# Final layer norm of a mixture-of-experts kernel: its rows loaded ahead of the last two blocks' adds, and those blocks' rows normed apart

## What is computed

```python
x = layernorm(x + time_mix(x))          # two recurrent layers
for e in range(8):                      # top-2 mixture of experts
    w_e = sum(probs * (top_i == e))     # weight 0 for rows not routed to e
    g = silu(x @ W1[e].T) * (x @ W2[e].T)
    out += (g @ W3[e].T) * w_e
x = layernorm(x + out)                  # the final norm
```

## Time and profile before

| | |
|---|---|
| median of 3 runs | 1149.59 us (1147.47 to 1152.86) |
| the profiled execution's own time | 1149.51 us |
| its span, first to last instruction | 1147.2 us |
| PE, DVE, ACT, POOL busy, share of the span | 92%, 79%, 55%, 57% |

### The profile page before, as it was taken

How to read it: one execution, slowest core, us unless ns; L and a number is a source line. 1 busy time by engine, 2 the same in 40 slices (tenths; PEclk the granted TensorE clock), 3 DMA queues, 4 the chain that set the end, 5 groups by cost and what they waited for, 6 DMA issues and landing times. The chain is left out here.

```text
span 1147.2 us, 22276 instructions
## 1 busy us (share of the span) xinstructions
PE 1052.3 (92%) x6690; PEld 925.1 (81%) x6690; DVE 903.2 (79%) x1990; ACT 633.2 (55%) x1101; POOL 657.2 (57%) x558
## 2 busy tenths in 40 slices
PE   6999999999999998789999999999999999999900
PEld 5788888787878786568888888888899999999900
DVE  5689998888888898676876677777778788888746
ACT  3455555555555554465454565565656666666528
POOL 2111545454555554565876777677658777777434
PEclk9899999999999999999999999999999999999955
DMA  4011221111121121556656877777778899899469
GB/s 185 19 46 65 56 56 57 56 55 55 55 55 55 55 56 38 179 137 183 134 107 182 193 199 205 186 215 186 217 192 203 241 268 234 241 252 242 83 219 385
DMA packets 81633, 167.74 MB, mean 146 GB/s; under 512 B 28224, under 2 KB 45504, under 8 KB 81312
## 3 DMA queue, kind: packets, MB, share of 16 engines
q1 hardware_dynamic: 51552, 131.41, 36.1%
q0 software_dynamic: 30016, 35.55, 16.6%
HBM read 121.82 MB, written 45.09 MB: 145 GB/s over the span
## 5 line engine op out<-in xcount | busy, mean ns | idle before, releaser
L883 POOL DMA_INDIRECT x_acc<-fy_sb,pair_out x135 | 251.5, 1863 | 115.3 <-issue 41.4
L1430 PE MATMUL ring<-fxh,fw_hi 128*128 128x256 f32 (+1 forms) x720 | 233.8, 325 | 3.6 <-ACT fxh L742 2.2
L1432 PE MATMUL ring<-fxh,fw_lo 128*128 128x256 f32 (+1 forms) x720 | 231.9, 322 | 0.0
L1431 PE MATMUL ring<-fxl,fw_hi 128*128 128x256 f32 (+1 forms) x720 | 231.7, 322 | 0.0
L637 ACT ACTIVATE fw_hi<-w_raw 128x1024 fp32r<-128x1024 f32 x162 | 169.8, 1055 | 78.7 <-PE out L1501 77.6
L969 DVE TENSOR_TENSOR fw_lo<-w_raw,fw_hi 128x1024 fp32r<-128x1024 f32 x162 | 196.6, 1219 | 14.7 <-ACT fw_hi L637 13.9
L103 POOL DMA_INDIRECT xg<-x_src,pair_in x135 | 156.9, 1162 | 67.4 <-issue 48.4
L811 POOL TENSOR_TENSOR rs<-ve,neg_half 128x4 f32<-128x4 f32 x48 | 55.7, 1160 | 225.4 <-DVE nm L920 225.4
L1251 PE MATMUL ring<-xh,w_hi 128*128 128x512 f32 x384 | 162.4, 423 | 3.9 <-issue 3.3
L93 POOL DMA_INDIRECT slot_list<-pairs,slot_u x128 | 133.8, 1046 | 46.7 <-issue 32.4
L1499 PE MATMUL out<-fw_hi,gh 128*128 128x256 f32 x540 | 153.9, 285 | 1.1 <-DVE slot_u L1028 1.1
(11 more groups left out here) (154 smaller groups left out, 1991.5 us busy)
## 6 DMA issues: line engine op xcount, KB each, us to landing
w_raw<-w_ffn SPq DMA_DIRECT2D x162, 512.0 KB, 4.9
x_in<-h SPq DMA_DIRECT2D x16, 512.0 KB, 3.2
x_src<-x SPq DMA_DIRECT2D x16, 512.0 KB, 4.3
x_acc<-x SPq DMA_DIRECT2D x16, 512.0 KB, 5.3
acc<-x_acc SPq DMA_DIRECT2D x16, 512.0 KB, 7.7
out<-o SPq DMA_DIRECT2D x16, 512.0 KB, 6.7
xg<-x_src,pair_in POOLq DMA_INDIRECT x135, 4.8
x_acc<-fy_sb,pair_out POOLq DMA_INDIRECT x135
```

The lines of the kernel that those rows point to most:

```text
L883: nc.gpsimd.indirect_dma_start(x_acc, bass.IndirectOffsetOnAxis(pair_out[j][:, q, 0:1].bitcast(U32), 0), fy[j][:, q, :], None, compute_op= ...
L1430: nc.tensor.matmul(out, hi, rows_hi, start=dc == 0, stop=False)
L1431: nc.tensor.matmul(out, hi, rows_lo, start=False, stop=False)
L1432: last = nc.tensor.matmul(out, lo, rows_hi, start=False, stop=dc == DC - 1)
```

## The change

`norm_phase` is gone, and its work stands at the end of `attention_and_experts`, on the same engines. Its 16 steps use no buffers of their own: `acc[0]` to `acc[15]` are tiles of the attention, free by then, and a step is normed in place.

- SP waits for the adds of blocks up to 51 only, loads steps 0 to 11 (`AHEAD`), stores steps 0 to 8 (`STORED`) as they are normed, and then waits for all adds. Then it loads steps 12 to 15, stores steps 9 to 11, waits for the four scatters below (`n_fixed`), and stores steps 12 to 15.
- POOL, ahead of the adds of block 52, takes the roots of steps 0 to 4 and waits until all twelve early loads have landed. Roots 5 to 10 stand between and behind the four adds.
- Rows of blocks 52 and 53 in steps 0 to 11 were loaded without those blocks' adds. So when all adds have landed POOL gathers these blocks' rows from `x_acc` (four indirect DMAs of 128 rows), they are normed as two short steps of two tiles (numbers 13 and 14 in the order of norms; the 18 norms are numbered 0 to 17, and steps 13 to 15 are norms 15 to 17), and POOL scatters them to `out` by four indirect DMAs, behind the stores of steps 0 to 11. Spare rows are left out of the scatter by its bound.

The core of the diff:

```diff
+AHEAD = 12
+STORED = 9
+FIX_AT = AHEAD + 1
+FINAL_DEPTH = 8
...
+            def store_out(n):
+                if n == AHEAD:
+                    sp.wait_ge(n_fixed, 64)
+                sp.wait_ge(n_o, final_no(n) + 1)
+                sp.dma_start(out_rows[n * CH:(n + 1) * CH, :].rearrange("(p q) d -> p q d", p=P),
+                             acc[n]).then_inc(n_out[n >= AHEAD], 16)
...
+            for b in (BLOCKS - 4, BLOCKS - 3):
+                sp.wait_ge(f_add[b % 2], 16 * sum(SIZES[b % 2:b + 1:2]))
+            for n in range(AHEAD):
+                load_acc(n)
+            for n in range(STORED):
+                store_out(n)
             for par in range(2):
                 sp.wait_ge(f_add[par], 16 * sum(SIZES[par::2]))
+            for n in range(AHEAD, STEPS):
+                load_acc(n)
+            for n in range(STORED, STEPS):
+                store_out(n)
...
+            for n in range(FIX_AT):
+                final_rows(n, acc[n])
+            for f in range(2):
+                final_rows(FIX_AT + f, fy[(BLOCKS + f) % 2])
+            for n in range(FIX_AT, STEPS):
+                final_rows(n + 2, acc[n])
...
+            def final_root(i):
+                j, tiles = i % FINAL_DEPTH, final_tiles(i)
+                pool.wait_ge(n_ve, i * 2 + 2)
+                if i >= FINAL_DEPTH:
+                    pool.wait_ge(n_o, i - FINAL_DEPTH + 1)
+                nc.gpsimd.tensor_tensor(fin_rs[:, j, 0:tiles], fin_ve[:, j, 0:tiles], neg_half[:, 0:tiles], ALU.pow).then_inc(n_rs, 1)
+                pool.wait_ge(n_rs, i + 1)
+                nc.gpsimd.tensor_tensor(fin_nb[:, j, 0:tiles], fin_rs[:, j, 0:tiles], fin_nm[:, j, 0:tiles], ALU.mult).then_inc(n_nb, 1)
...
+                    if at(s, BLOCKS):
+                        for i in range(5):
+                            final_root(i)
+                        for n in range(AHEAD):
+                            pool.wait_ge(n_in[n], 16)
+                    if at(s, BLOCKS + 1):
+                        final_root(7)
                     if within(s, 3, BLOCKS + 1):
                         pool.wait_ge(f_add[1 - j], spot.moved(-3))
                     pool.wait_ge(f_yv, spot.before(OUT_BANKS, -1))
...
+                        if at(s, BLOCKS) or at(s, BLOCKS + 1):
+                            final_root(5 + 3 * (s - BLOCKS) + q)
+                            pool.sem_inc(f_met, 1)
...
             run_experts(pool, xstep)
+            final_root(10)
+            for par in range(2):
+                pool.wait_ge(f_add[par], 16 * sum(SIZES[par::2]))
+            gather_final(0, 0)
+            final_root(11)
+            gather_final(0, 1)
+            gather_final(1, 0)
+            gather_final(1, 1)
+            for i in range(12, FIX_AT + 3):
+                final_root(i)
+            pool.wait_ge(n_o, FIX_AT + 2)
+            pool.wait_ge(n_out[0], 16 * AHEAD)
+            for f in range(2):
+                for q in range(2):
+                    scatter_final(f, q)
+                final_root(FIX_AT + 3 + f)
...
-        norm_phase(nc, x_acc, out)
```

More of the change, by code:

```diff
@@ L21 @@
+import math
 from contextlib import ExitStack
@@ L72 @@
 GATE = P // Q
+STEPS = TOKENS // CH
+AHEAD = 12
+STORED = 9
+FIX_AT = AHEAD + 1
+FINALS = STEPS + 2
+FINAL_DEPTH = 8
 def within(s, low, high):
@@ L209, in rest_starts, with attention_and_experts @@
     skips(nc, dve, k, 2)
-def attention_and_experts(nc, h, w_att, ln_wb, w_gate, w_ffn, x_src, x_acc, slot_list, kept):
+def attention_and_experts(nc, h, w_att, ln_wb, w_gate, w_ffn, x_src, x_acc, slot_list, out, kept):
     ident, w_raw_all, base, table = kept.ident, kept.w_raw, kept.base, kept.table
@@ L349, in attention_and_experts, with rows_in, in_decay, final_tiles @@
         f_wlo = [sem(f"wlo_ready{i}") for i in range(3)]
+        out_rows = out.rearrange("r (q d) -> (r q) d", q=Q)
+        def rows_in(buf):
+            flat = buf.rearrange("p a b c -> p (a b c)") if len(buf.shape) == 4 else buf.rearrange("p a b -> p (a b)")
+            return [flat[:, first:first + Q * D].rearrange("p (q d) -> p q d", q=Q)
+                    for first in range(0, flat.shape[1], Q * D)]
+        acc = [rows for buf in (k_sb, kv, state[0], state[1], r_sb[0], r_sb[1], y[0], y[1], u, z, x1, x1T, w_out, xg[0])
+               for rows in rows_in(buf[:])]
+        def in_decay(first, *shape):
+            n = math.prod(shape)
+            names = " ".join("abc"[:len(shape)])
+            return decay[:, first:first + n].rearrange(f"p ({names}) -> p {names}",
+                                                       **dict(zip("abc", shape)))
+        fin_stats, fin_mv = in_decay(0, FINAL_DEPTH, Q, 6), in_decay(192, FINAL_DEPTH, Q, 2)
+        fin_ve, fin_nm, fin_rs, fin_nb = (in_decay(256 + 32 * i, FINAL_DEPTH, Q) for i in range(4))
+        n_in = [sem(f"acc_loaded{i}") for i in range(STEPS)]
+        n_fix, n_fixed = [sem("fix_rows0"), sem("fix_rows1")], sem("fix_stored")
+        n_out = [sem("early_rows_stored"), sem("late_rows_stored")]
+        n_bn, n_mv, n_ve, n_rs, n_nb, n_o = (sem("final_stats"), sem("final_mean_var"), sem("final_var_eps"), sem("final_rstd"),
+                                             sem("final_norm_bias"), sem("final_rows"))
+        n_met = sem("final_waits_met")
+        def final_tiles(i):
+            return 2 if FIX_AT <= i < FIX_AT + 2 else Q
+        def tiles_to(i):
+            return sum(final_tiles(k) for k in range(i + 1))
+        def final_no(n):
+            return n if n < FIX_AT else n + 2
         block = ctx.enter_context(nc.Block())
@@ L541, in xstep, with load_acc @@
                     pairs(spot, -1, pair_out, 1 - j, f_pair_out[1 - j])
+            def load_acc(n):
+                sp.dma_start(acc[n], x_acc[n * CH:(n + 1) * CH, :].rearrange("(p q) d -> p q d", p=P)).then_inc(n_in[n], 16)
+            def store_out(n):
[4 more added lines that the diff above has]
+                             acc[n]).then_inc(n_out[n >= AHEAD], 16)
             run_experts(sp, xstep)
@@ L545, in _ @@
             sp.wait_ge(s_padst, 64)
+            for b in (BLOCKS - 4, BLOCKS - 3):
[4 more added lines that the diff above has]
+                store_out(n)
             for par in range(2):
                 sp.wait_ge(f_add[par], 16 * sum(SIZES[par::2]))
+            for n in range(AHEAD, STEPS):
+                load_acc(n)
+            for n in range(STORED, STEPS):
+                store_out(n)
+            sp.wait_ge(n_out[0], 16 * AHEAD)
+            sp.wait_ge(n_out[1], 16 * (STEPS - AHEAD))
+            sp.wait_ge(n_fixed, 64)
         @block.scalar
@@ L775, in xstep, with final_rows @@
                     probs(CHUNKS + 2, CHUNKS // 2 + 1, 0)
+            def final_rows(i, rows):
+                j = i % FINAL_DEPTH
+                act.wait_ge(n_nb, i + 1)
+                for q in range(final_tiles(i)):
+                    last = nc.scalar.activation(rows[:, q, :], rows[:, q, :], ACT.Identity,
+                                                bias=fin_nb[:, j, q:q + 1], scale=fin_rs[:, j, q:q + 1])
+                last.then_inc(n_o, 1)
             run(act, step)
             run_experts(act, xstep)
+            nc.scalar.activation(warm[:, :], neg_half[:, :], ACT.Identity)
+            for n in range(FIX_AT):
[4 more added lines that the diff above has]
+                final_rows(n + 2, acc[n])
         @block.gpsimd
@@ L861, in step, with gather_final, scatter_final @@
                 scatter(s, j, 7, 1)
+            def final_root(i):
[6 more added lines that the diff above has]
+                nc.gpsimd.tensor_tensor(fin_nb[:, j, 0:tiles], fin_rs[:, j, 0:tiles], fin_nm[:, j, 0:tiles], ALU.mult).then_inc(n_nb, 1)
+            def gather_final(f, q):
+                par = (BLOCKS + f) % 2
+                pool.sem_inc(n_met, 1)
+                nc.gpsimd.indirect_dma_start(
+                    fy[par][:, q, :], None, x_acc,
+                    bass.IndirectOffsetOnAxis(pair_out[par][:, q, 0:1].bitcast(U32), 0)).then_inc(n_fix[f], 16)
+            def scatter_final(f, q):
+                par = (BLOCKS + f) % 2
+                pool.sem_inc(n_met, 1)
+                nc.gpsimd.indirect_dma_start(
+                    out_rows, bass.IndirectOffsetOnAxis(pair_out[par][:, q, 0:1].bitcast(U32), 0),
+                    fy[par][:, q, :], None, bounds_check=TOKENS - 1, oob_is_err=False).then_inc(n_fixed, 16)
             def xstep(s, half, j, spot):
@@ L1199, in xstep, with final_stats @@
                     fill_table(nc, dve, kept, 2)
+            def final_stats(i, rows):
+                j, tiles = i % FINAL_DEPTH, final_tiles(i)
+                for q in range(tiles):
+                    nc.vector.bn_stats(fin_stats[:, j, q, :], rows[:, q, :]).then_inc(n_bn, 1)
+                dve.wait_ge(n_bn, tiles_to(i))
+                if i >= FINAL_DEPTH:
+                    dve.wait_ge(n_nb, i - FINAL_DEPTH + 1)
+                dve.sem_inc(n_met, 1)
+                for q in range(tiles):
```

(16 more changed lines are left out.)

## The result

The changed kernel takes 1161.88 us (four runs, 1161.11 to 1162.37), the kernel before 1150.53 beside it: 1.010 times as long, 95% interval 1.0074 to 1.0126. Forecast were 1158 us, a range of 1150 to 1166, and slower with a chance of 0.68. The profiled execution took 1162.37 us with a span of 1159.4.

A forecast was written before the change was run, and what follows sets the result against it. The end was taken as 12.7 us of waiting, then a norm with DVE, ACT and DMA near their limit; early loads to 1106.2, adds 9.4 + 7.8 to 1123.4, then 32.1 us, span 1155.5, plus 2.3 outside: 1158 us, range 1150 to 1166.

The forecast's parts named there:

- The early loads: SP's loads of steps 0 to 11: start at 1087.8, 14.8 us earlier than before, the twelfth landing at 1106.2.
- The hold: POOL, before block 52's adds: waiting for the twelve early loads moves the first add from 1088.64 to 1106.2, 17.6 us.
- The adds: POOL's adds of blocks 52 and 53: 9.4 and 7.8 us, all landed at 1123.4 (bounds 1121.8 and 1128.0).
- From there to the end: From all adds landed at 1123.4: gathers, short norms, scatters, last four stores in series, 32.1 us, last store ending at 1155.1.
- the quiet adds: Adds in the quiet end of the kernel before, landing after 4.7 us; taken as the price of the scatters' landing.
- One sign: In the changed profile: DMA engines nearly idle around 1120 and again near 1145.
- Rival A: Not slower: four serial landings of indirect transfers (two blocks' adds, gathers, scatters) are quick, 8.5 us less, 1149.5 us; chance 0.17.
- Rival B: Faster: transfers bound the end, adds and fix run beside a full stream, 1137 us; chance 0.08.
- Rival C: Slower still: every indirect transfer at the end runs as under load, adds 10.9 us a block, 1167 us; chance 0.15.

The follow-up runs named there:

- The run with roots behind: The changed kernel with roots 5 and 8 behind the second add of their block, not between its two adds: 1161.09 us, again 1160.35 us.
- the run with the adds freed: The changed kernel with the last two blocks' adds sent to `x_src`, not waiting for the loads, fix kept, 3 stores before late loads: 1156.88 us.

## Why the prediction was right

A single number in brackets is the forecast's.

**The early loads** went as forecast: from 1087.59 (1087.8), the twelfth landed at 1093.05 + 13.7 = 1106.75 (1106.2).

**The hold** was where I put it, and so was its size: 19.2 us for the first add (1088.64 to 1107.80), 17.6 forecast. One us of the difference is POOL's own, between the last landing at 1106.75 and its issue.

**The adds.** From block 52's first add to block 53's 9.93 us (9.4), and from there to the late loads 7.43 (7.8). All adds had landed by 1125.16 (1123.4). In the first block it was for the most part POOL's order and not the load that set the pace: 1.78 us lay between root 5 and the second add, where I had 0.3, and the root's first half took 1.63 us beside the add's issue instead of 1.01. The run with roots behind shows 7.87 us in the same place. So the 9.4, a middle taken because of the load, came near by luck.

**From there to the end.** Here two terms were off, on opposite sides. The gathers took 6.2 to 6.8 us to land, where I had 4.8 and 5.8 at most; I had taken them from gathers beside the experts' weights, and these ran beside the late loads and two stores. The forecast had the DMA engines idle for the most part there, though the end of the adds releases its own late loads together with the gathers: their share was 0.97 from 1124 to 1136. With POOL's gaps, root 15 ended 18.5 us behind the adds' end instead of 15.1. The scatters landed 2.4 us after their issue, not 4.7: the quiet adds were the wrong row for them, a plain transfer the right one. Counted from the adds' end, the last scatter landed at +27.3 (25.3), and the last store 6.5 us later at 1159.0 (6.4); ACT's last norm was not quite under the scatters' cover, for SP waited 0.4 us for it ahead of the last store. In all 3.9 us over the forecast's span, and 3.0 us outside the span instead of 2.3: that is the difference between 1158 and 1162. The number is as near as this because the errors of the gathers and the scatters cancel in part.

**One sign did not come.** The DMA engines were to be nearly idle around 1120, because ACT waits for POOL's roots; their share was 0.75 from 1106 to 1124, and 0.89 from 1118 to 1122. They stood nearly idle for a longer stretch once, behind 1136, not twice.

**Rival A** was right in one of its four terms, the scatters. The estimate of 2.3 us from "DMA: Bandwidth & Descriptors" in the Trainium skill (section "Anatomy of one DMA — SWDGE (gpsimd) path") agrees with their 2.4 us; for gathers the measurements are 3.2 us with the late loads left out and 6.6 beside them, and for adds 3.9 at best (1121.25 to 1125.16). **Rival B** asked for adds and fix beside a full stream; the DMA share of 0.18 from 1136 to 1150 is its end. **Rival C** had the load right for the gathers and in no other term.

What the forecast did not have is the balance: a start 15 us earlier is worth only 8 us, the hold takes 9, and the fix adds 12 to 13. In the versions tried, removing the hold or the fix alone does at best no more than come back to the time of before.

## What to carry to other kernels

Work that is pulled ahead of a serial tail has to leave the tail where it was: here the early loads took the place of the adds on POOL and in the DMA queues, and what the loads won (8 us) the adds lost (9 us). A repair of what was read too early belongs on the bill as a chain of its own, and a chain behind all adds and ahead of the last stores adds to the time link by link. Price an indirect transfer by a row with the same neighbours in the DMA queues: the same gather took 3.2 or 6.6 us.

## What the runs showed of the hardware that was not expected

A plain indirect scatter of 128 rows of 1 KB on idle DMA engines landed 2.4 us after the start of its issue, about as fast as a plain store of four times the bytes (2.6). An accumulating one landed after 4.7 us in the quiet end of the kernel before (DMA share 0.36), after at most 3.9 between stores of the changed kernel (1121.25 to 1125.16; share 0.75 from 1106 to 1124), and after 10.0 beside the 512 KB loads of the run with the adds freed.

An indirect DMA that follows a root on POOL at once started 0.5 to 1.8 us after it (1.78 and 0.54 in the changed kernel), while one behind another indirect DMA started 0.3 us after it. The trace names only issue as the cause, and no run here settles it.
